# Graph attention and experts on one core: TensorE signals its row sums four at a time, and the spread goes ahead of them

## The reference

```python
e = jax.nn.leaky_relu(al_s[src] + al_d[dst], NEG_SLOPE)
m = jax.lax.stop_gradient(jax.ops.segment_max(e, dst, num_segments=n))
ex = jnp.exp(e - m[dst])
denom = jax.ops.segment_sum(ex, dst, num_segments=n)
alpha = ex / (denom[dst] + 1e-16)
out = jax.ops.segment_sum(h[src] * alpha[:, :, None], dst, num_segments=n)
```

## Time and profile before

| what | value |
|---|---|
| runs | 5947.86, 5979.73 and 5987.34 us |
| median | 5979.73 us |
| profiled execution, its own time | 5986.06 us |
| its span, first to last instruction | 5984.3 us |
| granted TensorE clock, mean share of full speed | 0.718 |

### The profile page before, as it was taken

The page is one execution under the profiler, slowest core; times in us unless marked ns, Lnnn a source line. Parts: engine busy times, 40 slices in busy tenths (PEclk is TensorE's granted clock), DMA queues, the critical chain, the costliest instruction groups (busy, mean ns, idle before and its releaser), DMA issues. The chain is left out here.

```text
span 5984.3 us, 75332 instructions
## 1 busy us (share of the span) xinstructions
PE 3536.1 (59%) x12591; PEld 2261.5 (38%) x12592; DVE 3403.5 (57%) x8833; ACT 1641.2 (27%) x3595; POOL 3345.6 (56%) x3631
## 2 busy tenths in 40 slices
PE   5555555555566555555555665565555655657994
PEld 4333333333333333333333333333333333434673
DVE  6655555555555555556555565565555555653344
ACT  4222222222222222222232333233233232321222
POOL 5556555555565555555555655555555555645422
PEclk7777767777766767666666667667767666668997
DMA  5344334344444333333444444444444444444324
GB/s 157 106 110 110 107 103 107 103 110 109 110 111 110 104 104 108 104 103 98 111 113 112 116 113 114 113 112 113 114 112 111 116 115 110 116 119 138 101 83 156
DMA packets 319707, 670.45 MB, mean 112 GB/s; under 512 B 75272, under 2 KB 151192, under 8 KB 319357
## 3 DMA queue, kind: packets, MB, share of 16 engines
q0 software_dynamic: 170848, 469.37, 29.5%
q1 hardware_dynamic: 148201, 199.90, 11.6%
q10 hardware_dynamic: 596, 0.53, 0.0%
HBM read 602.38 MB, written 75.12 MB: 113 GB/s over the span
## 5 line engine op out<-in xcount | busy, mean ns | idle before, releaser
L1078 POOL DMA_INDIRECT rows<-table,idx x3200 | 3025.5, 945 | 2134.7 <-issue 913.4
L1225 PE MATMUL bank<-rows,hit 128*128 128x260 f32 (+1 forms) x6464 | 2586.4, 541 | 2131.3 <-issue 1217.8
L1225 PEld LDWEIGHTS bank<-rows,hit 128*128 128x128 f32 x6464 | 1491.3, 259 | 2986.5 <-issue 1687.4
L1333 DVE TENSOR_TENSOR acc<-acc,bank 128x260 f32 (+1 forms) x3232 | 1357.6, 420 | 1646.3 <-remote 855.7
L1320 DVE TENSOR_TENSOR rows<-rows,bank 128x1024 f32<-128x1024 f32 x808 | 946.1, 1212 | 12.5 <-ACT rows L1111 7.6
L1108 ACT ACTIVATE arg<-arg 128x32 f32<-128x32 f32 (+1 forms) x404 | 88.4, 219 | 3135.0 <-DVE arg L1313 2238.8
L1287 DVE TENSOR_TENSOR hit<-bank,dst_loc 128x256 f32<-128x256 f32 x1616 | 672.3, 417 | 86.7 <-issue 72.1
L1102 ACT ACTIVATE hit_t<-gap,ones 128x1024 bf16<-128x1024 bf16 x404 | 463.8, 1148 | 20.2
L1097 ACT ACTIVATE gap<-loc,minus_node 128x1024 bf16<-128x1024 bf16 x404 | 462.6, 1145 | 11.5 <-DMA loc<-loc_row 11.3
L1214 PE MATMUL bank<-du,hit_t 128*128 x3232 | 362.3, 180 | 113.4 <-issue 80.3
L1214 PEld LDWEIGHTS bank<-du,hit_t 128*128 128x128 bf16 x3232 | 275.5, 100 | 324.6 <-issue 229.1
(11 more groups left out here) (253 smaller groups left out, 2120.2 us busy)
## 6 DMA issues: line engine op xcount, KB each, us to landing
loc<-loc_row SPq DMA_DIRECT2D x404, 256.0 KB
rows<-table,idx POOLq DMA_INDIRECT x3200
sent<-zeros SPq DMA_DIRECT2D x202, 68.3 KB
xe<-sent SPq DMA_DIRECT2D x106, 128.5 KB
got<-back SPq DMA_DIRECT2D x96, 128.0 KB, 3.5
fw<-in_L_ffn_W SPq DMA_DIRECT2D x16, 512.0 KB, 8.9
table<-acc POOLq DMA_DIRECT2D x49, 130.0 KB
table<-acc SPq DMA_DIRECT2D x49, 128.5 KB
```

The source lines that it names most:

```text
L1078: pool.indirect_dma_start(rows[:, way, n, 0:R], None, table, bass.IndirectOffsetOnAxis(idx[:, way, n:n + 1], 0)).then_inc(rows_in[way], 16)
L1225: nc.tensor.matmul(sum_bank[n % 4][:, 0:R], hit[:, way, n, :], rows[:, way, n, 0:R], start=True, stop=True).then_inc(summed, 1)
L1333: nc.vector.tensor_tensor(kp.acc[:, t, 0:R], kp.acc[:, t, 0:R], sum_bank[n % 4][:, 0:R], ALU.add).then_inc(added, 1)
```

## The change

TensorE's `summed` counts two for a step instead of eight: one signal on sum 3 and one on sum 7. All who wait for it count in these units. The spread of step s + 2 moves from between the halves to ahead of sums 0 to 3, and has no signal of its own except in the first two steps; who waited for `spread` now waits for the signal of the first half behind it. The order of VectorE, ScalarE, GpSimd and SyncE stays.

```diff
@@ gpsimd: gather, with freed starting at 2 and growing by 2
-                        pool.wait_ge(summed, (s - SETS + 1) * ST)
+                        pool.wait_ge(summed, (s - SETS + 1) * 2)
@@ scalar: make_hit_t
-                    if not early(s):
+                    if number(s) and 2 <= s < 4:
                         act.wait_ge(spread, s - 1)
+                    if not number(s) or s >= 4:
+                        act.wait_ge(summed, s * 2 - 7)
@@ tensor: spread_du
-                    last.then_inc(spread, 1)
+                    if early(s):
+                        last.then_inc(spread, 1)
@@ tensor: sum_rows
-                def sum_rows(s, way, chunks):
-                    for n in chunks:
-                        if n % PIECE == 0:
-                            pe.wait_ge(scaled, s * PIECES + n // PIECE + 1)
+                def sum_rows(s, way, half):
+                    pe.wait_ge(scaled, s * PIECES + half + 1)
+                    for n in range(half * PIECE, (half + 1) * PIECE):
                         if not number(s) or s * ST + n >= 4:
                             pe.wait_ge(added, s * ST + n - 3)
-                        nc.tensor.matmul(sum_bank[n % 4][:, 0:R], hit[:, way, n, :], rows[:, way, n, 0:R],
-                                         start=True, stop=True).then_inc(summed, 1)
+                        last = nc.tensor.matmul(sum_bank[n % 4][:, 0:R], hit[:, way, n, :], rows[:, way, n, 0:R],
+                                                start=True, stop=True)
+                    last.then_inc(summed, 1)
@@ tensor: step
                     ride(way, turn)
-                    sum_rows(s, way, range(0, 4))
                     if not number(s) or s + 2 < STEPS:
                         spread_du(s + 2, (way + 2) % SETS)
-                    sum_rows(s, way, range(4, ST))
+                    sum_rows(s, way, 0)
+                    sum_rows(s, way, 1)
@@ vector: keep_du
-                    dve.wait_ge(spread, s + 1)
+                    if early(s):
+                        dve.wait_ge(spread, s + 1)
+                    else:
+                        dve.wait_ge(summed, s * 2 - 3)
@@ vector: add_sum
-                    dve.wait_ge(summed, s * ST + n + 1)
+                    dve.wait_ge(summed, s * 2 + n // PIECE + 1)
```

More of the change, by code:

```diff
@@ L1063, in _ @@
                 freed = pool.alloc_register(f"pool_rows_freed_{layer}")
-                pool.reg_mov(freed, ST)
+                pool.reg_mov(freed, 2)
                 def gather(s, way, turn):
@@ L1069, in gather @@
                     if not number(s):
-                        rows_freed = pool.snap(freed, min_val=ST, max_val=ITEMS)
+                        rows_freed = pool.snap(freed, min_val=2, max_val=2 * STEPS)
                     pool.wait_ge(idx_ready, s + 1 - AHEAD)
@@ L1073, in gather @@
                         pool.wait_ge(summed, rows_freed)
-                        pool.reg_add(freed, freed, ST)
+                        pool.reg_add(freed, freed, 2)
                     elif s >= SETS:
-                        pool.wait_ge(summed, (s - SETS + 1) * ST)
+                        pool.wait_ge(summed, (s - SETS + 1) * 2)
                     for n in range(ST):
```

## The result

The changed kernel took 6603.75 us (median of 4 runs, 6602.85 to 6612.81), the kernel before, on the same chip, 5963.8 (4 runs, 5930.28 to 5987.34): ratio 1.105 [1.100, 1.110], slower by about 640 us where I forecast 5575.

A forecast was written before the change was run, and what follows sets the result against it. The edge phases were taken as bound by waits, TensorE's signals being held while gathers flow. 5984.3 - 645 + 180 + 60 = 5579 us of span, 5581 as execution; profiled 6 us above the median, so 5575 us, range 4980 to 6050.

The forecast's parts named there:

- Part 1: TensorE's edge-phase signals: sending 2 instead of 9 a step removes the later waits of each half, saving 645 us.
- the 645 us: VectorE's 215 later waits of a half step, over 1 us each, ahead of adds and `keep_du`, all taken as saved.
- Part 2: Add 4 waits for sum 7 instead of sum 4: 0.9 us a step, 364 us in all, 180 taken.
- the two crept signals: TensorE signals seen singly by VectorE in one step, after 3.94 and 4.08 us of idling, taken as what halves usually show.
- rival 1: TensorE's deliveries wait until gathers pause, however few the signals; nothing saved, 6220 us, up to 6600; chance 0.17.
- Part 3: Spread ahead of sums 0 to 3 on TensorE: just fits, except with rides; 0 to 260 us, 60 taken.
- the 4.91 us: VectorE's time from add 4 to the next add 0, into which spread and four sums, 4.0 to 4.6 us, should fit.
- None at adds 5 to 7: Sign on VectorE: at most one long wait per half step, at adds 0 and 4, none at the others.
- `keep_du` without waits: Sign on VectorE: the waits ahead of `keep_du`, 362.1 us before, are gone afterwards.
- "Remote" down from 1218 by a third: Sign on VectorE: "remote" waits ahead of the adds and `keep_du` lines fall from 1218 us by a third or more.
- A new idle ahead of the fifth add: Sign on VectorE: 0.6 to 1.2 us of new idling ahead of the fifth add in quiet steps.
- GpSimd's 732.4 lower: Sign on GpSimd: its 732.4 us of waiting for the sums that free its sets gets lower.

The follow-up runs named there:

- e18: Kernel before with, in layer 1, only the spread in front; in layer 2, one signal per four sums, two waits a step, spread in its old place: 6219.27 against 5990.63 us.
- e7: The changed kernel with half of the gathers left out: 4319.26 us, against 3934.66 for the kernel before with the same half left out.
- e17: Kernel before with, in layer 1, adds waiting for complete groups only; in layer 2, the change with two waits a step: 6214.55 against 6018.86 us.
- e13: Kernel before with one more, already met wait at each add, where the kernel before takes about 5970: 6104.4 against 5977.9 us, 1.020.
- e2: Kernel before with one more, already met wait at each add, where the kernel before takes 4800: 4802.64 against 4802.29 us, 1.000.
- e5: The changed kernel itself, in a series where the kernel before takes 4800: 4805.66 against 4798.5 us, 1.0015.
- e10: Kernel before with half the gathers and adds waiting for their half's last sum, every sum signalled: 4397.4 us, in a series where the kernel before took 5976.11.
- e9: Kernel before with eight more loads of 32 KB a step on SyncE's queue: 4816.75 us in one run, the kernel before 4810.07.
- e4: Kernel before with only the spread moved in front of sums 0 to 3, all signals kept: 4802.14 against 4802.29 us, 1.000.

## Why the prediction was wrong

**Part 1 failed, and it carried the sign.** "They exist only because a second, third or fourth signal had to get through": with four signals made one in layer 2 of e18, the layer took 18 us longer instead of some 320 shorter, which half of the 645 us would have been. The 18 us hold part 2's cost as well, at most 182 us in a layer by the prediction's 0.9 a step, so part 1 saved at most some 165 us there. The layer's waits over 0.3 us ahead of adds and `keep_du` went from 861 to 1049 us, 783 of them now at the fifth add. In e18's first layer the spread's signal and four sums' came out within 0.17 us (1515.758 to 1515.928): where held signals come in such a burst, merging them saves nothing. The prediction took the two crept signals of the earlier trace rows as the rule, and their waits as the signals' alone; part of the 645 us was VectorE's own instructions, as the sixth to eighth adds show. That signals are not what sets the length of a wait is rival 1's mechanism, which I gave 0.17.

**Part 2's full price was sized right.** 0.9 us a step forecast, 0.95 measured in e7 without cover, for the whole change, but with 494.5 us of the adds' waits on TensorE; and 1.40 us from add 3 to add 4 inside the 1.28 to 1.81. Of its 364 us I took 180 as uncovered; e17 shows none in layer 1 (-64).

**Part 3 was mis-sized, and this is where the loss is.** I took 60 us and at most 260; it cost 213 in layer 1 alone (e18) and, with the shared signal, 270 in layer 2 (e17 against e18), 483 together. Its sum was off too: 4.6 us and a ride of 1.93 miss the 4.91 us by 1.6, not 1.3, so the bound should have been some 330 us, still under 483. The working counted TensorE's time ("so it just fits") and not the place of the signals. Argued from the timelines, not shown by a run: in the old order sums 0 to 3 often gave their signals before a hold began, and only the spread and what followed was held, for which VectorE could wait at `keep_du` (212 us in layer 1) with adds done. In front, the spread's matmuls and signal pass first, and sums 0 to 3 fall into the hold. In e18's first layer sum 0 ended 0.64 us after the end of the previous step's last add on the mean; before, 0.93 us ahead of it. In the changed kernel it ended 1.25 us ahead, because the adds themselves came later, so there the account doesn't rest on this.

**A term was missing.** The diff changes the number that an add waits for from one that `added` shares to another, and VectorE handled six more instructions a step for it: 14259 waits, register operations and the like in the edge phases instead of 11829 (all instructions: 77761, before 75332). I called the changed numbers of ScalarE's and GpSimd's waits free and didn't price VectorE's. 94 us of 408 in the second layer by e13, 119 by e17; nothing measurable where the kernel before takes 4800 (e2). It isn't simply their count: e13 has about as many instructions that take 0.62 us or more (1512, the changed kernel 1527, the kernel before 689) and lost only 2%.

**What the profile after was to show.** "None at adds 5 to 7": wrong, 760 us. `keep_du` without waits: right. "Remote" down from 1218 by a third: 1057.6, by 13%. A new idle ahead of the fifth add: right, 432 us in 274 waits for TensorE. GpSimd's 732.4 lower: 1802.0. Rival 1 gave 6220 us, up to 6600 with its costs wholly on the path; the measured 6603.75 is at that end, but by luck rather than by that sum: by the runs it is not part 2's costs uncovered, but part 3's order and the added instructions. The range, 4980 to 6050, left it out.

**Open.** What holds TensorE's signals while gathers flow, and what slows VectorE's register instructions. The Trainium skill ("NOTIFIC — the notification-queue block", 7.1 Overflow: three behaviours, one of which stalls the engine) says that the block's pipeline presses back rather than lose a record, which can stall an engine; no run here shows whether it is this. But the traces hold a sign that points at the recording itself. Where the kernel before takes 4800 us, nearly every count that an instruction raises has its record (16702 of 16702 in e2, all 13878 in e5). Where it takes 5970, a third of the records are missing: 11229 of 16702 in the kernel before, 9606 of 13878 in the changed kernel, 11260 of 15490 in e18; with half the gathers there, about a fifth (13209 of 16702 in e10). So records do get lost, where the trace doesn't say, and in just the series with the long time. Every time in this document was measured with that recording on; no run shows the kernels without it, and the 640 us may belong to it in part or wholly. Why the kernel before takes 4800 us in some series and 5970 in others is open as well: the same chips gave both, and more transfers (e9) didn't bring it about. Complete groups alone (-64 in one layer of one profile) may be a gain under that condition; they weren't run in both layers there, and they cost 0.1% elsewhere. No kernel with all its gathers was clearly faster than the one before.

## What to carry to other kernels

Where signals of an engine are held for many microseconds, look at their order before their number: here moving one ahead of the sums cost 213 us in a layer, and sending a quarter of them changed 18. Put first the work whose signal the critical engine waits for first. Before a run of late waits is put down to late signals, look for one that stands behind an event already seen, as the sixth to eighth adds here; that one is the waiting engine's own. Read the waiting engine's register instructions too, and compare the number of recorded signals with the number sent: where records are missing, the recording is one of the suspects. Price a changed wait expression by the instructions that it adds in the loop.

## What the runs showed of the hardware

- Under the 5970 condition TensorE's signals came as late as 13.3 us after the matmul (1502.62 to 1515.93 in e18, for sum 3) while GpSimd's gathers ran, some 3 us after the last gather's end; one for each sum (e18) and one for four (1535.65 to 1546.86 in the changed kernel) alike. Five held ones then came 0.04 us apart.
- In the same condition, instructions of VectorE between its operations take 0.62 to 1.5 us, 1527 of 14259 in the changed kernel; where the kernel before takes 4800 it was at most 8 in most runs, 33 in e9 and 52 in e4.
- In the same condition a third of the records of raised counts are missing from the trace (11229 of 16702 in the kernel before), and stamps of register instructions can be over 1.9 us late (1517.92, for one that the program has ahead of an add at 1515.97).
- With gathers whole and no holds, all edits of the edge phase lie within 0.2%; with half the gathers the same change costs 384.6 us of 3934.66. What sets the pace decides what a part is worth.
